# Query and projection on four 64x64 quadrants, with a group's images crossed between partition halves

## The chip, the cores and the metric

One core of one Trainium2 chip. The metric is device time in microseconds (us), from the start of the program to its end; several executions are timed and the median is compared. All data is float32.

## What is computed

A block of a convolutional network over 32 images of 64 channels and 16x16 pixels. Every step adds to its input:

```
x = x + conv_bn(x, dw0, groups=C)             # depthwise 3x3
x = x + ffn(x, f0)                            # 64 -> 128 -> relu -> 64
x = x + windowed_attn(x, ...)                 # 7x7 windows
x = x + conv_bn(x, dw1, groups=C)
x = x + ffn(x, f1)

def attn(xw):                                 # xw: windows, 49 tokens, 64 channels
    q = xw @ wq.T;  k, v = split(xw @ wkv.T);  k = k + pos
    q = focus((relu(q) + 1e-6) / sc);  k = focus((relu(k) + 1e-6) / sc)
    q, k, v = 4 heads of 16 channels
    z = 1 / (q . sum(k) + 1e-6)
    y = (q @ (k.T @ v)) * z + depthwise 5x5 of v
    return y @ proj_w.T + proj_b
focus(t) = t**3 / norm(t**3) * norm(t)
```

## The kernel before

The images go in eight groups of four. A group's tile has 128 partitions: channels of two images (index a, the partition half) times two images side by side in the columns (index j). So the four images of a group are (a, j). A window grid of 7x7 leaves four full windows of an image and a rest (right and bottom strips of 60 pixels).

**Slots.** Work is written out by hand for each engine, in slots n. Slot n runs the convolution and FFN of group n (of the first block; from slot 9 on, which has number n-1, those of the second block; slot 8 has none), queries, keys and values of group n-1, the key norms and key-value sums of groups n-2 and n-3, attention (attend, then take_y) of group n-5, y's turn to channels (turn_y) of group n-6, and the projection of group n-7. Slots 1 to 4 fill this up, with the convolution one group ahead. From slot 11 the rest of attention and the second block's end are written out singly.

**Order in a slot, PE** (TensorE; slots 6 to 10): conv, key_value_full, project, ffn1, attend, a window_conv in some (5, 6, 9), then query and ffn2 (in slots 5 and 6 ffn2 first), kv_rest, key_value_rest, q_norms, turn_y, kv_full. In slots 1 to 4: ffn1, conv, query, kv_full, kv_rest, key_value_rest, q_norms, ffn2.
**VectorE** (5 to 10): norm2, take_kv_full, norm6, ratios, take_y, k_focus, q_first, second, k_rest, k_full, k_guard, take_kv_rest. **ScalarE** (5 to 11): k_square, first, take_projected, k_sixth, hidden, take_fm, q_sixth, root, second, take_q_norms, take_v_rest, take_yt, take_v_full, q_square. **GpSimd** (POOL): add_pads, cube_k, third, y_sum, v_masks, cube_q. Each engine runs its list strictly in order; semaphores join them.

**Query** (L702, matmuls L719): for each partition half a one matmul of 64x64 weights over the 512 columns of both images, from half a to the same half of one PSUM bank (P_B + 1). **Project** (L875, L886) does the same into a spare convolution bank (groups 0 to 3) or P_B + 1. fp32 matmuls appear as two instructions each. So two of the four 64x64 quadrants of the array are in use. kv_full (L723, L734), kv_rest (L738), key_value_full (L780), key_value_rest (L800), attend (L808) and q_norms run over QUADRANTS (L139), all four.

**PSUM** has eight banks: 0 and 1 alternate for convolution and FFN output, P_H = 2, 3 hold the hidden layer, key rests and query norms, P_A = 4, 5 keys, values and attention, P_B = 6, 7 query, key-value sums, window convolution and turn_y. A step that reuses a bank waits for the engine that read it last.

**Afterwards.** q_first (L1045) takes the query from PSUM on VectorE; third adds the projection to x2, on POOL for groups 0 to 3 (L381, after ScalarE's take_projected, L523) and on VectorE for 4 to 7 (L1118). SP, the DMA queue, writes the result to mid in DRAM (L317) and reads it back by rows (L296) for the second convolution.

Of the kernel before, what the change touches and what calls it, by code (L numbers as in the profile page):

```python
# [8 lines left out]
ALU = mybir.AluOpType  # L9
# [126 lines left out]
def window_block_kernel(nc, x, taps_in, weights, consts, tables, out):  # L136
# [12 lines left out]
    with ExitStack() as ctx:  # L149
# [64 lines left out]
        vfull = sb("vfull", 128, NG, 8, VC)  # L214
# [7 lines left out]
        fm = sb("fm", 128, 2, NG, 4, C)  # L222
# [40 lines left out]
        def proj_bank(c):  # L263
            return spare(c + 7) if c < 4 else P_B + 1
# [70 lines left out]
        def _(eng):  # L335
# [37 lines left out]
            def y_sum(c):  # L373
                eng.wait_ge(y_ready, c + 1)
                eng.wait_ge(fm_ready, 3 if c < 4 else 6)
                full = y[:, c % 2, 0:8, :].rearrange("p (x s) c -> p x (s c)", x=2)
                eng.tensor_tensor(full, full, fm[:, :, c].rearrange("p x s c -> p x (s c)"), ALU.add)  # L377
# [35 lines left out]
        def _(eng):  # L413
# [19 lines left out]
            def take_v_full(g):  # L433
                eng.wait_ge(full_ps, g + 1)
                eng.wait_ge(kfull_ready, g + 1)
                eng.activation(vfull[:, g, :, 0:C], bank(P_A, 2).rearrange("p (s c) -> p s c", c=128)[:, :, C:128], ACT.Copy,  # L436
                               scale=cc("mask0")).then_inc(v_ready, 1)
# [64 lines left out]
            def take_fm(e):  # L502
# [3 lines left out]
                if part < 2:  # L506
                    for wx in range(2):
                        src = bank(P_B + wx).rearrange("p (d s h) -> p s d h", d=8, h=NH)
                        dst = fm[:, wx, gs, :, 32 * part:32 * part + 32].rearrange("p g s (d h) -> p (g s) d h", h=NH)
# [13 lines left out]
            def take_projected(c):  # L523
# [3 lines left out]
                eng.activation(xw[:, c % 2].rearrange("p j n -> p (j n)"), bank(proj_bank(c)), ACT.Identity,  # L527
# [92 lines left out]
        def _(eng):  # L620
# [4 lines left out]
            def conv(m, n, js=slice(0, GP)):  # L625
# [9 lines left out]
                if 0 <= n - 8 < 4:  # L635
                    eng.wait_ge(xw_ready, n - 7)
# [16 lines left out]
            def ffn1(m, n):  # L653
# [11 lines left out]
                if 0 <= n - 2 < NG:  # L665
                    eng.wait_ge(krest_ready, n - 1)
                if m == 13:
                    eng.wait_ge(y_ready, NG)
# [33 lines left out]
            def query(g, n):  # L702
# [14 lines left out]
                for a in range(2):  # L717
                    p = slice(64 * a, 64 * a + 64)
                    last = eng.matmul(bank(P_B + 1)[p].rearrange("p (j n) -> p j n", j=GP), ww("wq")[p], x2[p, g, :, 0:PX],  # L719
                                      start=True, stop=True)  # L720
# [17 lines left out]
            def kv_rest(g, n):  # L738
                eng.wait_ge(x2_ready, g + 1)
                if n < 5:  # L740
# [39 lines left out]
            def key_value_full(g, n):  # L780
# [10 lines left out]
                for j in range(GP):  # L791
                    for wy in range(2):
                        s = 2 * j + wy
                        for a, wx in QUADRANTS:
                            p = slice(64 * wx, 64 * wx + 64)
                            last = eng.matmul(bank(P_B + wx)[64 * a:64 * a + 64, VC * s:VC * s + VC], kf[p, g % 2, a, s, :],  # L796
                                              vfull[p, g, 4 * a + s, :], start=True, stop=True)
                last.then_inc(kvx_ps, 1)

            def key_value_rest(g):  # L800
                eng.wait_ge(vm_ready, g + 1)
                for a, j in QUADRANTS:
                    p = slice(64 * j, 64 * j + 64)
                    last = eng.matmul(bank(P_H + j)[64 * a:64 * a + 64, 0:5 * VC], kf[p, g % 2, a, 4, :],
# [553 lines left out]
```

## Time and profile before

| | |
|---|---|
| median of 3 runs | 174.64 us (173.4 to 175.21) |
| profiled execution | 174.51 us, span 172.7 us |
| PE busy | 157.2 us (91%) |
| VectorE, ScalarE, GpSimd busy | 103.9, 83.7, 57.5 us |
| mean granted clock of TensorE | 0.98 |
| DMA | 18.77 MB, mean 109 GB/s |

The span runs from the first to the last instruction of the profile; the execution's own time is longer by what lies around it. Shares of busy time are means over the whole span: the slots have different limits, so the rows below are read slot by slot. In a timeline a group's time is from its first start to its last end, and the next group can start before that end.

### The profile page before, as it was taken

How to read it: one execution, taken by the hardware profiler on the slowest of the kernel's cores; microseconds unless marked ns; L12 is line 12 of the kernel's file. 1: busy time of each engine (PE TensorE's matmuls, PEld its weight loads, DVE VectorE, ACT ScalarE, POOL GpSimd, SP SyncE). 2: the span in 40 equal slices, each digit the busy share in tenths (PEclk: the TensorE clock that was granted, in tenths of full speed). 3: DMA queues.
4: the chain of work that ended last, by engine and by line, in shares of the span. 5: the costliest groups of instructions: out<-in, count | busy, mean ns of one | idle time of the engine just before them, and what ended most of it. 6: DMA issues, size and time to landing. Idle time of an engine off the chain costs nothing. (4 is left out here: it accounts for less than half of the span.)

```text
span 172.7 us, 6668 instructions
## 1 busy us (share of the span) xinstructions
PE 157.2 (91%) x2840; PEld 76.6 (44%) x2840; DVE 103.9 (60%) x270; ACT 83.7 (48%) x178; POOL 57.5 (33%) x75
## 2 busy tenths in 40 slices
PE   6977999899898999999996789999989999987893
PEld 3312252627274873583383562576433425222231
DVE  1168263858777778597588586582189476606043
ACT  2054869494937665756745414653431414033132
POOL 4000028260825504263934926640254312000000
PEclk9999999999999999999999956999999999999999
DMA  5999999940000000000054161063027181959943
GB/s 144 291 245 292 212 215 208 206 84 6 0 4 4 4 4 4 0 4 4 28 141 78 66 143 35 4 171 72 4 76 163 63 173 66 189 167 218 299 140 121
DMA packets 18028, 18.77 MB, mean 109 GB/s; under 512 B 1104, under 2 KB 17744, under 8 KB 17872
## 3 DMA queue, kind: packets, MB, share of 16 engines
q1 hardware_dynamic: 17568, 17.83, 44.6%
q10 hardware_dynamic: 432, 0.52, 1.1%
q8 instruction: 22, 0.36, 0.9%
q14 instruction: 6, 0.05, 0.1%
HBM read 14.16 MB, written 4.19 MB: 106 GB/s over the span
## 5 line engine op out<-in xcount | busy, mean ns | idle before, releaser
L649 PE MATMUL ps<-xc,dwf 96*32 96x480 f32 (+3 forms) x408 | 44.9, 575 | 3.4 <-DMA xc<-mid 2.4
L371 POOL TENSOR_TENSOR qt<-q 128x512 f32<-128x512 f32 x8 | 10.7, 1333 | 57.2 <-ACT q L465 57.2
L649 PEld LDWEIGHTS ps<-xc,dwf 96*32 96x32 f32 x408 | 12.1, 112 | 32.7 <-issue 24.2
L424 ACT ACTIVATE x<-ps,wts 128x512 f32<-128x512 f32 x15 | 10.3, 685 | 26.0 <-PE ps L649 26.0
L671 PE MATMUL ps<-x,w1s 64*128 64x512 f32 x60 | 16.7, 637 | 2.9 <-DVE kvm L1107 1.4
L431 ACT ACTIVATE hid<-ps,wts 128x512 f32<-128x512 f32 x27 | 17.2, 682 | 3.2 <-PE ps L671 3.2
L677 PE MATMUL ps<-hid,w2s 128*64 128x512 f32 x60 | 17.2, 614 | 0.0
L377 POOL TENSOR_TENSOR y<-y,fm 128x512 f32<-128x512 f32 x8 | 10.2, 1274 | 10.7 <-DVE y L1161 7.7
L1061 DVE TENSOR_REDUCE nrm<-k 128x10 f32<-128x640 f32 x8 | 6.6, 819 | 11.6 <-ACT k L459 11.5
L358 POOL TENSOR_TENSOR k<-k 128x640 f32<-128x640 f32 x8 | 12.4, 1550 | 3.4 <-ACT k L453 3.4
L734 PE MATMUL ps<-wts,x 64*64 64x128 f32 x256 | 11.2, 294 | 0.6 <-DVE y L1161 0.6
L760 PEld LDWEIGHTS ps<-cst,q 64*64 64x64 f32 x512 | 10.8, 135 | 1.5 <-ACT q L473 0.9
L760 PE MATMUL ps<-cst,q 64*64 64x1 f32 x512 | 10.1, 192 | 0.3 <-ACT q L473 0.3
L734 PEld LDWEIGHTS ps<-wts,x 64*64 64x64 f32 x256 | 8.7, 143 | 3.5 <-issue 3.5
L719 PE MATMUL ps<-x,wts 64*64 64x512 f32 x32 | 8.6, 612 | 1.7 <-DVE kvm L1094 1.4
L364 POOL TENSOR_TENSOR vm<-vrest,cst 128x640 f32<-128x640 f32 x8 | 10.1, 1268 | 0.0
L671 PEld LDWEIGHTS ps<-x,w1s 64*128 64x128 f32 x60 | 4.6, 184 | 10.9 <-ACT x L424 5.8
L1112 DVE TENSOR_SCALAR hid<-ps,wts 128x512 f32<-128x512 f32 x3 | 2.3, 751 | 11.7 <-PE ps L671 11.6
L1094 DVE TENSOR_TENSOR kvm<-ps,cst 128x544 f32<-128x544 f32 x8 | 5.7, 717 | 5.6 <-PE ps L796 5.6
L1107 DVE TENSOR_TENSOR kvm<-ps,cst 128x680 f32<-128x680 f32 x8 | 6.9, 859 | 3.1 <-issue 2.3
L436 ACT ACTIVATE vfull<-ps,cst 128x512 f32<-128x512 f32 x8 | 5.5, 686 | 6.6 <-DVE kraw L1025 6.6
L459 ACT ACTIVATE k<-k 128x640 f32<-128x640 f32 x8 | 5.9, 736 | 5.7 <-POOL k L358 5.7
(139 smaller groups left out, 277.7 us busy)
## 6 DMA issues: line engine op xcount, KB each, us to landing
xc<-in_x SPq DMA_DIRECT2D x16, 240.0 KB, 11.4
xc<-mid SPq DMA_DIRECT2D x16, 240.0 KB, 4.7
xc<-in_x SPq DMA_DIRECT2D x8, 256.0 KB, 10.7
mid<-x SPq DMA_DIRECT2D x8, 256.0 KB, 2.2
xc<-mid SPq DMA_DIRECT2D x8, 256.0 KB, 3.3
out<-x SPq DMA_DIRECT2D x7, 256.0 KB, 5.7
tab<-in_tables SPq DMA_DIRECT2D x1, 1024.0 KB, 11.4
wts<-in_weights SPq DMA_DIRECT2D x1, 644.0 KB, 7.2
```

The lines of the kernel that those rows point to most:

```text
L358: eng.tensor_tensor(k3[:, :], k2[:, :], k1[:, :], ALU.mult).then_inc(k3_ready, 1)
L364: eng.tensor_tensor(vm[:, g % 2, :, :, 0:C], vrest[:, g].unsqueeze(2).broadcast_to([128, 2, 5, C]), cc("mask5").unsqueeze(1).unsqueeze(3). ...
L371: eng.tensor_tensor(qt[:, g % QB, 0:GC], q2[:, g % 2, 0:GC], q1[:, :], ALU.mult).then_inc(qt_ready, 1)
L377: eng.tensor_tensor(full, full, fm[:, :, c].rearrange("p x s c -> p x (s c)"), ALU.add)
L424: eng.activation(x1[:, m % 2, :], bank(m % 2), ACT.Identity, bias=ww(f"dwb_{m // NG}")).then_inc(x1_ready, 1)
L431: eng.activation(hid[:, m % 2, a, :], bank(hidden_bank(m) + a), ACT.Relu, bias=ww(f"fb1_{m // NG}")).then_inc(h_ready[a], 1)
L649: last = eng.matmul(out_ps[32 * q:32 * q + 32, :, :, to], dwf[:, s, q % 2, i, :], src[:, :, :, of], start=(i == 0), stop=False, skip_group ...
L671: eng.matmul(bank(hidden_bank(m) + a), w1s[p, s, :], x1[p, m % 2, :], start=True, stop=True).then_inc(h_ps, 1)
L677: last = eng.matmul(bank(m % 2)[64 * a:64 * a + 64], w2s[:, s, :], hid[:, m % 2, a, :], start=False, stop=True, skip_group_check=True)
L719: last = eng.matmul(bank(P_B + 1)[p].rearrange("p (j n) -> p j n", j=GP), ww("wq")[p], x2[p, g, :, 0:PX], start=True, stop=True)
L734: last = eng.matmul(bank(P_A + a)[64 * wx:64 * wx + 64, 128 * (2 * j + wy):128 * (2 * j + wy) + 128], x2[64 * a:64 * a + 64, g, j, at:at + ...
L760: eng.matmul(bank(P_H + a)[64 * h:64 * h + 64, at:at + 1], src[p, of:of + 64], one[p], start=True, stop=True)
```

## The change

Query and project run over all four quadrants, 256 columns each. A quadrant that leads from half a to half r carries image j = a ^ r, so two of the four images change their half between query and projection; project crosses them back. q is then spread over banks P_B and P_B + 1, 256 columns in each, and the projection over two banks: P_H, P_H + 1 for groups 0 to 3, a spare convolution bank with P_B + 1 for 4 and 5, P_A, P_A + 1 for 6 and 7. Key-value sums go to crossed halves, and vfull, fm and the window convolution's operands are reordered to match.

The waits follow the banks: turn_y waits for q_first of its slot, project for the last users of P_H, ffn1 for take_projected, convolutions 11 and 12, project(7) and ffn1(13) for third. In PE's order attend moves ahead of ffn1 in slots 6 to 10; in VectorE's, q_first moves ahead of take_y (slots 7 and 8) or directly behind it (slots 5 and 6).

```diff
-        def proj_bank(c):
-            return spare(c + 7) if c < 4 else P_B + 1
+        def proj_banks(c):
+            if c < 4:
+                return P_H, P_H + 1
+            return (spare(9 + c), P_B + 1) if c < 6 else (P_A, P_A + 1)
...
-                eng.activation(vfull[:, g, :, 0:C], bank(P_A, 2).rearrange("p (s c) -> p s c", c=128)[:, :, C:128], ACT.Copy,
+                eng.activation(vfull[:, g // 4, :, g % 4, 0:C], bank(P_A, 2).rearrange("p (s c) -> p s c", c=128)[:, :, C:128], ACT.Copy,
...
-                eng.activation(xw[:, c % 2].rearrange("p j n -> p (j n)"), bank(proj_bank(c)), ACT.Identity,
+                eng.activation(xw[:, c % 2], bank(P_H, 2).rearrange("p (j n) -> p j n", j=GP)[:, :, 0:PX], ACT.Identity,
...
(conv)
-                if 0 <= n - 8 < 4:
-                    eng.wait_ge(xw_ready, n - 7)
+                if m in (11, 12):
+                    eng.wait_ge(x3_ready, m - 6)
...
(ffn1)
+                if 0 <= n - 7 < 4:
+                    eng.wait_ge(xw_ready, n - 6)
                 if m == 13:
-                    eng.wait_ge(y_ready, NG)
+                    eng.wait_ge(x3_ready, NG)
...
(query)
-                for a in range(2):
-                    p = slice(64 * a, 64 * a + 64)
-                    last = eng.matmul(bank(P_B + 1)[p].rearrange("p (j n) -> p j n", j=GP), ww("wq")[p], x2[p, g, :, 0:PX],
-                                      start=True, stop=True)
+                for a, r in QUADRANTS:
+                    j = a ^ r
+                    last = eng.matmul(bank(P_B + j)[64 * r:64 * r + 64, 0:PX], ww("wq")[64 * a:64 * a + 64],
+                                      x2[64 * a:64 * a + 64, g, j, 0:PX], start=True, stop=True)
...
(kv_rest)
+                if n == NG:
+                    eng.wait_ge(xw_ready, 2)
...
(key_value_full)
-                            last = eng.matmul(bank(P_B + wx)[64 * a:64 * a + 64, VC * s:VC * s + VC], kf[p, g % 2, a, s, :],
-                                              vfull[p, g, 4 * a + s, :], start=True, stop=True)
+                            last = eng.matmul(bank(P_B + wx)[64 * (a ^ j):64 * (a ^ j) + 64, VC * s:VC * s + VC], kf[p, g % 2, a, s, :],
+                                              vfull[p, g // 4, 4 * a + s, g % 4, :], start=True, stop=True)
...
(window_conv)
-                            src = vfull[p, gs, :, NH * dc:NH * dc + NH].rearrange("p g (a j y) h -> p (g a) j y h", a=2, j=2)[:, :, j]
+                            src = vfull[p, half, :, :, NH * dc:NH * dc + NH].rearrange("p (a j y) g h -> p a j (y g) h", a=2, j=2)
+                            src = src[:, ::-1, j] if j else src[:, :, j]
...
(turn_y)
+                if n <= NG:
+                    eng.wait_ge(q_ready, n)
...
(project)
                 if c < 4:
-                    eng.wait_ge(x2_ready, nextconv(n) - 1)
-                else:
+                    eng.wait_ge(kvr_ready, n - 3)
+                    eng.wait_ge(qn_ready, min(n - 2, NG))
+                    eng.wait_ge(krest_ready, min(n - 1, NG))
+                elif c < 6:
+                    eng.wait_ge(x2_ready, c + 6)
                     eng.wait_ge(kvx_ready, NG)
                     eng.wait_ge(fm_ready, 6)
-                    if c > 4:
+                    if c == 5:
                         eng.wait_ge(x3_ready, c)
-                for a in range(2):
-                    p = slice(64 * a, 64 * a + 64)
-                    last = eng.matmul(bank(proj_bank(c))[p], ww("proj")[p], yt[p, c % 2, :], start=True, stop=True)
+                else:
+                    eng.wait_ge(y_ready, NG)
+                    if c == 7:
+                        eng.wait_ge(x3_ready, c)
+                for r, a in QUADRANTS:
+                    j, p = r ^ a, slice(64 * r, 64 * r + 64)
+                    last = eng.matmul(bank(proj_banks(c)[j])[64 * a:64 * a + 64, 0:PX], ww("proj")[p],
+                                      yt[p, c % 2, PX * j:PX * j + PX], start=True, stop=True)
...
(PE's order)
                         project(n - 7, n)
+                    attend(n - 5, n)
                     if m is not None:
                         ffn1(m, n)
-                    attend(n - 5, n)
...
(q_first)
-                eng.tensor_scalar(q1[:, :], bank(P_B + 1), 0.0, ecol[:, 0:1], ALU.max, ALU.add).then_inc(q_ready, 1)
+                eng.tensor_scalar(q1[:, :].rearrange("p (j n) -> p j n", j=GP), bank(P_B, 2).rearrange("p (j n) -> p j n", j=GP)[:, :, 0:PX],
+                                  0.0, ecol[:, 0:1], ALU.max, ALU.add).then_inc(q_ready, 1)
...
(VectorE's order)
                 ratios(n - 2)
+                if n in (7, 8):
+                    q_first(n - 1)
                 take_y(n - 5)
+                if n in (5, 6):
+                    q_first(n - 1)
                 if n - 2 < NG:
                     k_focus(n - 2)
-                if n - 1 < NG:
-                    q_first(n - 1)
```

## Rows read from the trace of the kernel before

**Rows 1.** The profile's first part: busy us, share of span, instructions.

```profile
PE 157.2 (91%) x2840; PEld 76.6 (44%) x2840; DVE 103.9 (60%) x270; ACT 83.7 (48%) x178; POOL 57.5 (33%) x75
```

**Rows 2.** Stretches, slots 7, 8: length, busy us (instructions), PE clock, DMA share, GB/s.

```profile
78.20:90.60 12.40, 12.40 (x274) 6.34 (x270) 9.44 (x22) 7.91 (x18) 7.51 (x10) 1.00 0.20 58
90.60:103.00 12.40, 9.12 (x242) 6.10 (x236) 9.38 (x22) 4.94 (x11) 7.51 (x10) 0.88 0.41 92
```

**Rows 3.** Stretches, columns as before, finer behind slot 8.

```profile
99.90:103.00 3.10, 2.48 (x42) 1.81 (x38) 2.64 (x8) 0.60 (x1) 0.47 (x1) 0.52 0.72 163
103.00:106.70 3.70, 3.70 (x24) 0.99 (x24) 3.11 (x4) 1.83 (x3) 1.50 (x3) 0.50 0.40 72
```

**Rows 4.** Waits of PE: us in total, times, longest us.

```profile
PE ps L719 <- DVE kvm L1094: 1.4, 1, 1.4
PE ps L671 <- DVE kvm L1107: 1.4, 2, 0.7
```

**Rows 5.** The chain that ended last, one piece: start, us, what.

```profile
144.12 2.15 DMA mid<-x
```

**Rows 6.** PE in time order: start, us, line, operation, count [idle before <-releaser].

```profile
21.79 0.65 PE L719 MATMUL ps<-x,wts 64*64 64x512 f32 x2
...
23.42 0.28 PE L747 MATMUL ps<-wts,x 64*64 64x128 f32 x2
...
61.17 0.65 PE L719 MATMUL ps<-x,wts 64*64 64x512 f32 x2 [0.30 <-ACT fm L510]
...
62.71 0.69 PE L760 MATMUL ps<-cst,q 64*64 64x1 f32 x31
...
86.53 0.45 PE L747 MATMUL ps<-wts,x 64*64 64x128 f32 x8
86.79 0.75 PE L804 MATMUL ps<-vm,kf 64*64 64x340 f32 x8
87.36 0.59 PE L760 MATMUL ps<-cst,q 64*64 64x1 f32 x32
...
108.01 1.02 PE L886 MATMUL ps<-yt,wts 64*64 64x512 f32 x4
108.97 1.13 PE L671 MATMUL ps<-x,w1s 64*128 64x512 f32 x4
```

**Rows 7.** PE in order of time, slots 6 to 8.

```profile
76.16 0.90 PE L773 MATMUL ps<-cst,y 128*64 128x98 f32 x16
...
89.62 1.10 PE L734 MATMUL ps<-wts,x 64*64 64x128 f32 x32
...
101.09 1.98 PE L734 MATMUL ps<-wts,x 64*64 64x128 f32 x32 [0.62 <-DVE y L1161]
```

**Rows 8.** VectorE in order of time, slots 6 to 8.

```profile
75.00 0.28 DVE L1161 TENSOR_TENSOR y<-ps,den 128x128 f32<-128x128 f32 x1
...
88.43 0.28 DVE L1161 TENSOR_TENSOR y<-ps,den 128x128 f32<-128x128 f32 x1
...
100.67 0.28 DVE L1161 TENSOR_TENSOR y<-ps,den 128x128 f32<-128x128 f32 x1
...
101.60 0.74 DVE L1049 TENSOR_SCALAR q<-ps,ecol 128x512 f32<-128x512 f32 x1
```

**Rows 9.** ScalarE in order of time, hidden layer of slots 9 and 10.

```profile
110.29 1.26 ACT L431 ACTIVATE hid<-ps,wts 128x512 f32<-128x512 f32 x2
...
124.47 1.26 ACT L431 ACTIVATE hid<-ps,wts 128x512 f32<-128x512 f32 x2 [0.36 <-PE ps L671]
```

**Rows 10.** PE in order of time, slots 9 and 10.

```profile
112.26 1.08 PE L677 MATMUL ps<-hid,w2s 128*64 128x512 f32 x4
...
123.31 1.13 PE L671 MATMUL ps<-x,w1s 64*128 64x512 f32 x4
...
125.51 1.35 PE L677 MATMUL ps<-hid,w2s 128*64 128x512 f32 x4
...
129.34 0.70 PE L823 MATMUL ps<-kvm,qt 64*64 64x68 f32 x32 [0.66 <-DVE y L1161]
```

More of the change, by code:

```diff
@@ L213, in window_block_kernel @@
         kf = sb("kf", 128, 2, 2, 5, C)
-        vfull = sb("vfull", 128, NG, 8, VC)
+        vfull = sb("vfull", 128, 2, 8, 4, VC)
         vrest = sb("vrest", 128, NG, 2, C)
@@ L221, in window_block_kernel @@
         y = sb("y", 128, 2, 10, C)
-        fm = sb("fm", 128, 2, NG, 4, C)
+        fm = sb("fm", 128, 2, 2, 4, 4, C)
         fmr = sb("fmr", 128, NG, 2, C)
@@ L375, in y_sum @@
                 eng.wait_ge(fm_ready, 3 if c < 4 else 6)
-                full = y[:, c % 2, 0:8, :].rearrange("p (x s) c -> p x (s c)", x=2)
-                eng.tensor_tensor(full, full, fm[:, :, c].rearrange("p x s c -> p x (s c)"), ALU.add)
+                full = y[:, c % 2, 0:8, :].rearrange("p (x s) c -> p x s c", x=2)
+                eng.tensor_tensor(full, full, fm[:, :, c // 4, :, c % 4], ALU.add)
                 rest = y[:, c % 2, 8:10, :]
@@ L508, in take_fm @@
                         src = bank(P_B + wx).rearrange("p (d s h) -> p s d h", d=8, h=NH)
-                        dst = fm[:, wx, gs, :, 32 * part:32 * part + 32].rearrange("p g s (d h) -> p (g s) d h", h=NH)
+                        dst = fm[:, wx, half, :, :, 32 * part:32 * part + 32].rearrange("p s g (d h) -> p (s g) d h", h=NH)
                         last = eng.activation(dst, src, ACT.Copy)
@@ L803, in key_value_rest @@
                     p = slice(64 * j, 64 * j + 64)
-                    last = eng.matmul(bank(P_H + j)[64 * a:64 * a + 64, 0:5 * VC], kf[p, g % 2, a, 4, :],
+                    last = eng.matmul(bank(P_H + j)[64 * (a ^ j):64 * (a ^ j) + 64, 0:5 * VC], kf[p, g % 2, a, 4, :],
                                       vm[p, g % 2, a].rearrange("p w c -> p (w c)"), start=True, stop=True)
@@ L860, in window_conv @@
                             last = eng.matmul(bank(spare(n))[p, 32 * dc:32 * dc + 32], trest[p, dc, :],
-                                              vrest[p, gs, :, NH * dc:NH * dc + NH].rearrange("p g a h -> p (g a) h"),
+                                              vrest[p, gs, ::1 - 2 * k, NH * dc:NH * dc + NH],
                                               start=True, stop=True)
@@ L1121, in third @@
                 eng.wait_ge(mid_out, 16 * (c - 1))
-                dst, src = x3[:, c % 2, :], bank(proj_bank(c))
+                dst = x3[:, c % 2, :]
                 for j in range(GP):
+                    src = bank(proj_banks(c)[j])
                     for wx in range(2):
-                        at = PX * j + 98 * wx
+                        at = 98 * wx
                         eng.scalar_tensor_tensor(natural(dst, j)[:, 0:14, WR * wx:WR * wx + WR],
@@ L1129, in third @@
                 for j in range(GP):
-                    at = PX * j + WIN
+                    src, at = bank(proj_banks(c)[j]), WIN
                     eng.scalar_tensor_tensor(natural(dst, j)[:, :, 14:16], src[:, at:at + 32].rearrange("p (h w) -> p h w", w=2),
@@ L1213, in _ @@
             eng.tensor_copy(ecol[:, :], bank(P_B)[:, 0:1]).then_inc(ecol_ready, 1)
-            eng.tensor_copy(vfull[:, :, :, C:VC].rearrange("p g s h -> p (g s) h"),
+            eng.tensor_copy(vfull[:, :, :, :, C:VC].rearrange("p b s g h -> p (b s g) h"),
                             cc("mask0").unsqueeze(2).broadcast_to([128, NG * 8, NH]))
```

## The prediction

> **What bounds the kernel now.** The page's first part comes first: TensorE (PE) is busy for 157.2 of 172.7 us [rows 1], so shorter matmuls look like time won. The second view, the stretches by slot, asks whether that holds everywhere. In slot 7 PE is busy for all 12.40 us; in slot 8, which has no convolution, for 9.12 of 12.40 [rows 2]. The reader should see that VectorE does 9.4 us in both, so slot 8 is as long as slot 7 with 3.3 us less of PE work: another chain sets its length. That chain is one group's keys: kv_full (PE), k_full and k_guard (VectorE), k_square (ScalarE), cube_k (GpSimd), k_sixth (ScalarE), norm6, ratios, take_y (VectorE), and back to the next kv_full, which waits for the last y. The third view is the granted clock: it was 0.52 and 0.50, the lower of its two levels, from about 99.9 to 106.7 us, just behind slot 8's idle time [rows 3]. Fourth, the waits of PE: query waits 1.4 us for VectorE's key-value copy (slot 8), ffn1 waits twice 0.7 us for the other one (slots 4 and 5) [rows 4]. Last, the chain that ended last: from 144.12 us on it is nearly all DMA, beginning with the write of group 5 to mid, which third(5) on VectorE releases [rows 5]. So the end moves by as much as project(5) and third(5) do, and what is saved behind them (projections 6 and 7) counts for nothing.
>
> **One query or projection.** Now four instructions of 512 columns run on two quadrants; project holds PE from 108.01 to 108.97, 0.96 us [rows 6]. After it, eight of 256 columns run on four. The nearest row is key_value_rest, eight instructions of 340 columns on four quadrants, 86.79 to 87.36: 0.57 us [rows 6]. 256 columns can't cost more if the four overlap as there, and in proportion they cost 0.43. I take 0.45, as the work is columns, and keep 0.43 to 0.57. A project so saves 0.5, and a query at most as much.
>
> One condition differs from key_value_rest: there each half of the array's rows has a bank of its own; here both halves write to each of the two banks, in different partition halves. The old project does the same, both halves into one bank, and its four instructions of 0.6 us mean overlap within 1.02 us [rows 6], so the sharing does not stop them. The Trainium skill ("TensorEngine Tiling (Array Packing)", Gotcha 1: PSUM Pressure) says that different row tiles cannot use one PSUM bank at the same time. By that rule the new pairs would take turns and each call would stay near 0.96 us; the row speaks against it, for disjoint partitions at least. It is rival 4.
>
> **Slots 1 to 4.** Before, kv_full already fills the quadrants that query leaves empty: from the first query matmul to the end of both is 23.42 - 21.79 = 1.63 us [rows 6], where kv_full alone lasts 1.10 [rows 7]. After: 0.45 + 1.10 = 1.55, less a little overlap at the seam (project lasts 1.02 and its successor starts after 0.96). I take 0.15 saved for each. Slots 2 and 3 are paced by VectorE, which comes to k_full only behind k_focus and q_first of the same slot, with PE waiting for its copies [rows 4], so two of the four reach the end: 0.3 (bounds 0.1 and 0.6).
>
> **Slot 5.** Query, kv_rest and key_value_rest take 62.71 - 61.17 = 1.54 us interleaved; the last two alone 87.36 - 86.53 = 0.83 [rows 6]. After: 0.45 + 0.83 = 1.28. Saved: 0.26.
>
> **Slot 6.** ffn2 is held by the hidden layer, which ScalarE reaches only behind k_sixth; moving attend ahead of ffn1 changes nothing there. Query would give 0.26 again, but turn_y now waits for q_first, since query writes its bank too, and behind turn_y stands kv_full. q_first follows take_y, which ends at 75.00 + 0.28, and lasts 0.74 [rows 8]: 76.02, where turn_y began at 76.16 [rows 7]. Saved: 0.15. k_focus moves back by 0.74; its reader, the next slot's key_value_full, has a whole convolution in front of it, so that costs nothing.
>
> **Slots 7 and 8.** q_first is moved ahead of take_y. It was already in VectorE's order, but behind the y that kv_full waits for; now it lies in front, inside the key chain. In slot 7 the last y was written at 88.71 [rows 8], so it comes at 89.45, and kv_full, which began at 89.62 [rows 7], gains 0.15 at most, though PE has 1.0 us less to do. In slot 8 kv_full was already waiting (0.62 us) for the y of 100.95 [rows 7, 8]; there 0.74 goes straight on the path. I take -0.7. The new waits of project in slot 8 (it must see the last key-value copy of slot 7) hold attend and query too, but query stood for 1.4 us anyway [rows 4], and 0.45 + 1.1 fits in that.
>
> **Slots 9 and 10.** attend now runs before ffn1, so ScalarE copies the projection under it (half of the 1.26 us that two such copies take [rows 9], under attend's 1.1, from ffn1's end at 124.44 to 125.51 [rows 10]) and ffn1's new wait costs nothing. But attend was also the cover of the hidden layer, 1.26 us of ScalarE between ffn1 and ffn2. Slot 9: project ends 0.5 earlier, ffn1 starts at 108.97 - 0.5 + 1.1 = 109.6 and ends at 110.7, hidden at 112.0, and ffn2 ends 1.1 later, as in slot 10 (126.86 against 125.73): 113.1 against 113.34 [rows 6, 9, 10]. Saved: 0.2. In slot 10 nothing else stands between ffn1 and ffn2: ffn1 starts 0.6 later, at 123.9, so ffn2 ends 0.6 later too. In return take_y starts 1.6 earlier, and the 0.66 us that attend(6) waited for it [rows 10] go. Net: 0.05.
>
> **Slots 11 and 12.** PE is busy throughout up to project(5); projections 4 and 5 give 0.5 each: 1.0. The new waits for third are covered: third(5) was done at 144.1 [rows 5], and the convolution that must wait for it stood behind four more PE steps. Copies, masks and the relabelled operands keep their element counts: 0.
>
> **Sum.** 0.3 + 0.26 + 0.15 + 0.15 - 0.7 + 0.2 + 0.05 + 1.0 = 1.4 us. The profiled execution took 174.51 us (span 172.7 plus 1.81 around it), 0.13 below the median shown; 174.51 - 1.4 = **173.1 us**.
>
> **Rivals.**
> 1. *The saving reaches the end everywhere.* PE is 91% busy. Four queries at 0.15, three at 0.26, one (slot 7, no interleaving) at 0.5 and six projections at 0.5 make 4.9: 169.6 us. Against it stands slot 8, where missing PE work did not shorten the slot. Chance 0.10.
> 2. *The slow clock goes or shrinks.* It cost kv_full 1.98 - 1.10 = 0.88 [rows 7], and 3.7 us at half rate behind it another 1.85 [rows 3]: 2.7. If the idle stretches fall otherwise, all of it may go: 173.1 - 2.7 = 170.4; half, 171.7. Against it: slot 8 idles more, not less. Chance 0.15.
> 3. *A second slow stretch, and slower.* Slot 7 loses 1.0 us of PE work and little of its length, so PE stands idle there as it did before the clock fell behind slot 8. It decides if the granted clock falls at the end of slot 7 too: that costs another 2.7, 175.8. Against it: by my sum slot 7 idles 0.9 us, slot 8 idled 3.3. Chance 0.15.
> 4. *The quadrants take turns.* Calls stay at 0.96, nothing is saved, and the reordering remains: in slot 7, 9 and 10 ffn1 comes 1.1 later (some 0.35, 0.3 and 0.45 lost), in slot 8 -0.7: 174.51 + 1.8 = 176.3. The old project speaks against it. Chance 0.07.
>
> **How the numbers follow.** The forecast has the other 0.53. Its own range: with 0.57 for a call the sum falls to about 0.5 (174.0); with nothing lost in slot 8 it is 2.1 (172.4); so 172.2 to 174.1. From 170.8 to 175.9 the range leaves out rival 1, rival 4 and the lowest part of rival 2, about 2 in 10. The runs before differ by about 1%, which is what can be told from no change: below 172.9 is faster, above 176.4 slower. Faster: rivals 1 and 2 and two fifths of the forecast, 0.46. Slower: half of rival 4, a little of rival 3, and 0.03 for what I don't see: 0.09. Same: 0.45.
>
> **What would show it.** Query and project at 0.43 to 0.57 us, all four quadrants overlapping; slots 7 and 8 each about 12.3 us from kv_full to kv_full, with PE waiting for y in both; attend(6) without a wait; ffn2 in slot 10 waiting for the hidden layer; third(5) about 1.4 us earlier. The prediction is wrong if slot 8 gets shorter at the full clock, if a stretch at 0.5 is missing or a second appears, or if third(5) moves and the end does not.

## The result, and the profile after

The changed kernel is a little slower. Its median is 178.16 us over 20 runs, 174.97 us for the kernel before in as many; the medians hold disturbed executions (12 of the changed kernel's 20), which the ratio leaves out: 1.0103, with a 95% interval of 1.0061 to 1.0145. The forecast of 173.1 us (170.8 to 175.9) missed. The profiled execution took 175.90 us with a span of 174.0 us, 1.3 us longer than the span before.

The page's first part and the granted clock in 40 slices (in tenths of full speed), changed kernel:

```profile
PE 154.8 (89%) x2904; PEld 78.5 (45%) x2904; DVE 102.8 (59%) x270; ACT 84.1 (48%) x178; POOL 57.4 (33%) x75
PEclk9999999999999999999999858999999999969999
```

PE is busy for 2.4 us less than in [rows 1], though it has 64 more matmuls and 64 more weight loads. The clock falls twice where it fell once. Stretches of the changed kernel, columns as in [rows 2]: slots 7 and 8, then the parts at the lower clock.

```profile
77.80:90.30 12.50, 12.26 (x294) 6.87 (x293) 9.48 (x23) 7.91 (x18) 7.52 (x10) 1.00 0.21 58
90.30:102.90 12.60, 8.69 (x244) 6.62 (x235) 9.32 (x22) 5.05 (x11) 7.51 (x10) 0.83 0.29 69
98.60:102.00 3.40, 2.77 (x36) 2.43 (x40) 3.25 (x12) 0.60 (x1) 1.24 (x2) 0.50 0.08 20
102.00:105.40 3.40, 3.40 (x36) 1.38 (x32) 2.12 (x3) 1.37 (x3) 0.09 (x1) 0.50 1.04 217
153.10:156.00 2.90, 2.88 (x16) 0.81 (x20) 0.00 (x0) 0.00 (x0) 0.00 (x0) 0.52 0.43 139
```

The stretch behind slot 8 answers to [rows 3]; the one at 153.1 is new. What PE did before it stands in its waits (us in total, times, longest; "issue" means that it waited for nothing that the profile shows), changed kernel:

```profile
PE ps L651 <- DMA xc<-mid: 3.2, 1, 3.2
PE ps L902 <- issue: 1.9, 1, 1.9
PE ps L681 <- ACT hid L433: 1.2, 3, 0.8
PE ps L651 <- issue: 0.5, 1, 0.5
```

PE stands once for 3.2 us, waiting for the rows that conv(13) reads back from mid; before, the same line had three waits, none over 1.0 us. The chain that ended last (start, us, what), changed kernel, says why those rows came late:

```profile
143.88 3.76 DMA mid<-x
...
148.50 4.57 DMA xc<-mid
...
153.12 4.37 PE ps L651 x24
```

third(5) releases the write of group 5 at 143.88, 0.24 us earlier than in [rows 5], but it lands after 3.76 us, not 2.15. The read behind it is late by that, and conv(13) starts behind the read and runs at the lower clock: 4.37 us, where a convolution at the full clock takes 2.68. The DMA view of the write, packets by queue, first the kernel before (144.0 to 147.5 us), then the changed one (143.8 to 147.7):

```profile
GB/s 0 0 0 0 0 0 0 0 0 0 0 94 293 363 363 339 363 351 351 316 153 12 0 0 0 0 0 0 0 0 0 0 0 0 0 0 47 82 82 23
q1 hardware_dynamic: 292, 0.28, 25.9%
```

```profile
GB/s 0 0 0 0 0 0 0 0 0 11 263 357 315 347 357 336 336 273 221 0 0 0 0 0 0 0 0 11 11 11 11 0 0 0 0 0 0 0 0 0
q1 hardware_dynamic: 272, 0.26, 20.2%
q8 instruction: 1, 0.02, 1.4%
```

The bulk of the write takes as long in both. In the changed kernel nothing of the write moves for some 0.8 us (each figure is a slice of 0.1 us) and then a trickle of 11 GB/s ends it: in the packets, 15 of the write's 16 shares (each ends with a packet of 4 bytes) have ended by 145.66 us and the last at 146.91, behind a 16 KB load of instructions on queue 8 (145.58 to 146.46 us). Over the whole program queue 8 has 23 such loads, 22 before. PE's stream, the list of instructions that it works off, has 2904 matmuls and as many weight loads now, 2840 of each before: an estimate of 250 to 260 such entries for a load.

PE in order of time, changed kernel, parts of slots 1, 6 to 8, 9 and 10, then the same part of slot 10 before:

```profile
22.71 0.66 PE L723 MATMUL ps<-x,wts 64*64 64x256 f32 x8
23.19 1.05 PE L738 MATMUL ps<-wts,x 64*64 64x128 f32 x32
...
75.74 0.90 PE L779 MATMUL ps<-cst,y 128*64 128x98 f32 x16 [0.27 <-DVE q L1066]
...
89.09 1.10 PE L738 MATMUL ps<-wts,x 64*64 64x128 f32 x32
...
101.20 1.98 PE L738 MATMUL ps<-wts,x 64*64 64x128 f32 x32 [0.55 <-DVE y L1180]
...
107.35 0.61 PE L902 MATMUL ps<-yt,wts 64*64 64x256 f32 x8
107.78 0.65 PE L829 MATMUL ps<-kvm,qt 64*64 64x68 f32 x32
...
118.20 1.04 PE L651 MATMUL ps<-xc,dwf 96*32 96x512 f32 x2
119.74 2.67 PE L651 MATMUL ps<-xc,dwf 96*32 96x512 f32 x22 [0.49 <-issue]
...
122.86 0.61 PE L902 MATMUL ps<-yt,wts 64*64 64x256 f32 x8
...
126.28 1.65 PE L681 MATMUL ps<-hid,w2s 128*64 128x512 f32 x4 [0.77 <-ACT hid L433]
```

```profile
119.23 2.68 PE L649 MATMUL ps<-xc,dwf 96*32 96x512 f32 x24
...
122.36 1.02 PE L886 MATMUL ps<-yt,wts 64*64 64x512 f32 x4
```

The calls are as short as forecast: query holds PE for 23.19 - 22.71 = 0.48 us, project for 107.78 - 107.35 = 0.43. But conv(9) breaks off after 2 of its 24 matmuls and goes on at 119.74: its two matmuls should have ended near 118.6, and no engine is named as the one that held it. From its start to project it takes 122.86 - 118.20 = 4.66 us, against 3.13 (122.36 - 119.23) before: 1.5 us lost in the middle of a convolution that no named wait holds. The 4,802nd entry of PE's stream (here semaphore instructions count too) is the one that comes late; a 16 KB load began at 116.91 and ended at 118.23. The 1.9 us of L902 in the waits above, in slot 8, are another matter: project goes on at 92.69 us, 0.10 us after VectorE has written the key-value copy that it waits for (91.73 to 92.59).

So the span's 1.3 us come from three parts. To the first convolution: 9.25 us against 8.26, +1.0. From there to the end of third(5): 134.61 (143.86 - 9.25) against 135.84, -1.2, with the broken conv(9) in it. From there to the end of the chain: 27.97 against 26.46, +1.5. The first part can't be put down to the change: one and the same kernel further down (the kernel before with fill, run twice) had its first convolution at 9.23 and at 8.40.

### The profile page after: what moved, and what is told of

Read it like the earlier page. It is cut to its first block and busy times, and to the rows that moved or that the text cites. A ratio compares the mean times of both kernels' runs of the same rounds, so it can differ in the third digit from the quotient of the medians.

```text
span 174.0 us, 6802 instructions
## 1 busy us (share of the span) xinstructions
PE 154.8 (89%) x2904; PEld 78.5 (45%) x2904; DVE 102.8 (59%) x270; ACT 84.1 (48%) x178; POOL 57.4 (33%) x75
## 5 line engine op out<-in xcount | busy, mean ns | idle before, releaser
L651 PE MATMUL ps<-xc,dwf 96*32 96x480 f32 (+3 forms) x408 | 46.7, 584 | 4.6 <-DMA xc<-mid 3.2
L651 PEld LDWEIGHTS ps<-xc,dwf 96*32 96x32 f32 x408 | 13.0, 114 | 34.4 <-issue 27.7
L681 PE MATMUL ps<-hid,w2s 128*64 128x512 f32 x60 | 18.4, 614 | 1.2 <-ACT hid L433 1.2
L379 POOL TENSOR_TENSOR y<-y,fm 128x512 f32<-128x512 f32 x8 | 10.2, 1269 | 11.9 <-DVE y L1180 8.9
L766 PEld LDWEIGHTS ps<-cst,q 64*64 64x64 f32 x512 | 9.8, 135 | 2.8 <-ACT q L475 1.3
L766 PE MATMUL ps<-cst,q 64*64 64x1 f32 x512 | 9.5, 192 | 0.7 <-ACT q L475 0.7
L738 PE MATMUL ps<-wts,x 64*64 64x128 f32 x256 | 9.5, 290 | 0.6 <-DVE y L1180 0.6
L675 PEld LDWEIGHTS ps<-x,w1s 64*128 64x128 f32 x60 | 4.6, 184 | 10.2 <-issue 6.9
L625 PE MATMUL ps<-x 128*128 128x512 f32 x12 | 7.9, 824 | 1.5 <-DVE x L1183 1.5
L738 PEld LDWEIGHTS ps<-wts,x 64*64 64x64 f32 x256 | 8.1, 144 | 1.7 <-issue 1.2
L523 ACT ACTIVATE yt<-ps 128x512 f32<-128x512 f32 x8 | 4.8, 597 | 8.4 <-PE ps L783 8.4
```

The costliest lines, as they stand in the source:

```text
L379: eng.tensor_tensor(full, full, fm[:, :, c // 4, :, c % 4], ALU.add)
L625: eng.matmul(bank(P_B + 1), x1[:, 0, 0:128], x1[:, 0, :], start=True, stop=True)
L651: last = eng.matmul(out_ps[32 * q:32 * q + 32, :, :, to], dwf[:, s, q % 2, i, :], src[:, :, :, of], start=(i == 0), stop=False, skip_group ...
L675: eng.matmul(bank(hidden_bank(m) + a), w1s[p, s, :], x1[p, m % 2, :], start=True, stop=True).then_inc(h_ps, 1)
L681: last = eng.matmul(bank(m % 2)[64 * a:64 * a + 64], w2s[:, s, :], hid[:, m % 2, a, :], start=False, stop=True, skip_group_check=True)
L738: last = eng.matmul(bank(P_A + a)[64 * wx:64 * wx + 64, 128 * (2 * j + wy):128 * (2 * j + wy) + 128], x2[64 * a:64 * a + 64, g, j, at:at + ...
```

## The experiments

The theory after the two traces: the slots gain as forecast, and it is lost again because the change adds 8 entries to PE's stream with each query and project (88 ahead of conv(9), 112 up to and with projection 5). So the instruction loads fall elsewhere: PE waits for one in conv(9), another delays the write of group 5, and behind that write the clock falls. The rivals: the lower clock alone (slot 8, tail), or the change's own order.

**The changed kernel again.**

> The changed kernel once more. Theory A (the clock): PE stands idle longer in slot 8 and before convolution 13, the granted clock falls to 0.5 in both places, and the stretches together cost more than the 1.4 us saved; ratio to before 1.005 to 1.02, and the profile has two stretches at 0.5, one from about 99 us and one from about 150 us. Theory B (order and DMA): the loss is the late landing of group 5's write (3.76 us instead of 2.15) and the pause of 1.2 us in convolution 9, both of which then show again, whatever the clock does.

Measured: 176.5 us, ratio 1.0144 [1.0087, 1.0201]. conv(9) breaks at the same matmul (118.35 x2, then 119.89), the write lands in 4.03 us, the clock falls in both places, conv(13) takes 5.13 us. So none of these is an accident of one execution.

**Hold the clock up.** Matmuls on constants into a free bank, in places where PE stands idle: in slot 8 (first), ahead of conv(13) and conv(14) (second), in both (third).

```diff
+            def fill(b, k):
+                for _ in range(k):
+                    eng.matmul(bank(b)[:, 0:PX], cc("ident"), tab[:, 0:PX], start=True, stop=True)
...
+                    if n == 8:
+                        fill(0, 4)
                     if n >= 7:
                         project(n - 7, n)
...
+            fill(P_B, 4)
             conv(13, 14)
...
```

> The changed kernel with seven extra matmuls of 256 columns (128x128 weights, constants, result never read) in PE's idle places of slot 8: four before project, one each before q_norms, turn_y and kv_full. Theory A: the clock stays high through slot 8 and convolution 8 runs in 2.7 us instead of 3.8 to 4.5; 2 to 2.7 us faster than the changed kernel, ratio to before about 0.995. Theory B: no faster than the changed kernel, slower by up to 0.5 us where a filler is longer than the wait.

> The changed kernel with four such matmuls between convolutions 12 and 13 and two before convolution 14, where PE waits for the rows read back from mid. Theory A: no stretch at 0.5 in the tail, convolution 13 in 2.7 us instead of 4.4; 1.5 to 2 us faster than the changed kernel. Theory B: the same time or slower by up to 0.5 us, since the DMA sets the end.

> The changed kernel with the fillers of slot 8 and of the tail together. Theory A: 3.5 to 4.5 us faster than the changed kernel, about 172 us, ratio to before about 0.985, and a mean granted clock above 0.98. Theory B: 0 to 1 us slower than the changed kernel.

Measured: 176.56 us, ratio 1.0078 [1.0028, 1.0128]; 175.86 us, 1.0105 [1.0054, 1.0156]; 175.45 us, 0.9966 [0.9918, 1.0014]. PE in order of time, first kernel:

```profile
102.05 2.68 PE L651 MATMUL ps<-xc,dwf 96*32 96x512 f32 x24
...
117.43 0.45 PE L858 MATMUL ps<-vfull,tab 64*64 64x64 f32 x11 [1.40 <-issue]
117.80 2.68 PE L651 MATMUL ps<-xc,dwf 96*32 96x512 f32 x24
```

All three gained less than expected. Each fill does its part and no more. With slot 8 filled, the convolution behind it runs at the full clock (2.68 us, where it began at the lower one in [rows 3]), but in the tail the clock still falls, and for longer: 10.2 us (149.9 to 160.1), 3.4 in the changed kernel's first profile. With the tail filled, conv(13) takes 2.68 us, but the clock falls in slot 8. With both the mean clock is 1.00, and by the ratios (1.0144 to 0.9966, same chip) that is worth 1.8%, 3.1 us. What the clock does not explain stays: the write lands in 3.73 to 4.18 us in all three. And with slot 8 filled the pause moves: the fill adds 28 entries ahead of it, so that the late entry no longer lies in conv(9) but in the window convolution just before it. It goes with the count of entries, not with a line of the program.

**Move the loads.** 43 one-column matmuls in place of one of the opening ones (172 entries for 4, as a float32 matmul is two matmul entries and two weight loads), in the changed kernel; the same with 29 in the kernel before; and with 36 and both fills in the changed kernel.

```diff
+            for i in range(43):
+                a, r = QUADRANTS[i % 4]
+                eng.matmul(bank(P_A + a)[64 * r:64 * r + 64, 0:1], x1[64 * a:64 * a + 64, 0, 0:64], x1[64 * a:64 * a + 64, 0, 0:1],
+                           start=True, stop=True)
-            for _ in range(6):
+            for _ in range(5):
```

> The changed kernel; one of the six opening matmuls is replaced by 43 of one column, so PE's stream holds 168 instructions more before its first convolution and every later instruction lies 168 places further on; nothing else is changed. Theory C (instruction loads): PE's instructions come in loads of 16 KB, 256 instructions each; one now falls on convolution 9 and one on group 5's write. Moved by 168 they fall elsewhere: convolution 9 without its pause (1.4 us), the write lands after about 2.2 us instead of 3.8 to 4.2, end 2 to 3 us earlier, ratio to before about 0.995 to 1.0. Theory A (the clock alone): pause and late landing stay, or their going changes nothing; ratio 1.01 to 1.015.

> The kernel before, its stream shifted in the same way by 112 instructions, as many as query and projection add up to project(5). Theory C: it takes on the changed kernel's loads: a pause of about 1.4 us in convolution 9 or the window convolution ahead of it, group 5's write landing after 3.7 us or later, 2 to 3 us slower than before, ratio 1.01 to 1.02. Theory A: ratio 1.00, since no work and no idle time of a slot is changed.

> The changed kernel with the fillers of slot 8 and the tail, and the stream shifted by 140 instructions ahead of the first convolution, so that with slot 8's 28 it lies 168 further on from convolution 9. Theories A and C together: clock high throughout, no pause, early landing: 5 to 6 us faster than the changed kernel, about 171 us, ratio about 0.975. Theory A alone: as with the fillers only, 0.997. Theory C alone: as with the shift only, about 0.995.

Measured: 175.11 us, ratio 0.9991 [0.9954, 1.0028]; 185.19 us, without a ratio; 177.46 us, 1.0145 [1.0093, 1.0198]. In the first, conv(9) is whole and the write lands in 2.14 us, PE in order of time:

```profile
10.64 2.68 PE L655 MATMUL ps<-xc,dwf 96*32 96x512 f32 x24
...
118.52 2.68 PE L655 MATMUL ps<-xc,dwf 96*32 96x512 f32 x24
```

It gains 1.1% on the changed kernel although its first convolution starts 1.4 us later; that delay came with the edit. The clock has a part in this, though: in this profile it stays at 1.00 in slot 8, though PE stands for 1.9 and 1.4 us there, and falls only in conv(13). The second has pauses of 1.8 and 1.2 us with the releaser "issue" in slot 3 and ahead of conv(9), and its write lands in 4.06 us, but it lost 10 us where 2 to 3 were expected, its first convolution began 2.5 us later, and the clock fell in four places: it settles nothing. The third missed as well: a pause of 1.9 us appeared in slot 3, in q_norms, with a stretch at the lower clock behind it. A shift that clears two places can put the pause in a third.

**Move the loads where PE is idle.** 18 one-column matmuls behind conv(0) and 24 behind conv(1), of constants, in the changed kernel (168 entries).

```diff
+            def tiny(k):
+                for i in range(k):
+                    a, r = QUADRANTS[i % 4]
+                    eng.matmul(bank(P_A + a)[64 * r:64 * r + 64, 0:1], cc("ident")[64 * a:64 * a + 64, 64 * a:64 * a + 64], cc("one")[64 * a:64 * a + 64],
+                               start=True, stop=True)
...
             conv(0, 0)
+            eng.wait_ge(c_in, 16)
+            tiny(18)
             ffn1(0, 0)
             conv(1, 1)
+            tiny(24)
```

> The changed kernel with 42 matmuls of one column (168 instructions) where PE waits anyway, behind its first two convolutions, instead of ahead of the first one; no other change. Theory C: the loads lie as with the shift before, without the 1.4 us that the shift cost at the start: conv 9 without a pause, write of group 5 landing after 2.2 us, ratio to before 0.985 to 0.995, and any rest above that is the clock's. Theory A alone: 1.01.

Measured: 173.22 us, ratio 0.9886 [0.982, 0.9953], 2.2% below the changed kernel by the ratios. PE in order of time and a piece of its chain:

```profile
118.77 2.68 PE L651 MATMUL ps<-xc,dwf 96*32 96x512 f32 x24
...
121.90 0.61 PE L902 MATMUL ps<-yt,wts 64*64 64x256 f32 x8
```

```profile
142.92 2.15 DMA mid<-x
```

The kernel has 42 useless matmuls more and is faster. conv(9) to project is 3.13 us again; the write lands in 2.15. The lower clock behind slot 8 is still there (99.0 to 105.8); the fall in the tail is gone without any fill: PE's longest wait for a read from mid is 2.0 us there, not 3.2. From the write of group 5 to the end of the chain it now takes 26.4 us, as in the kernel before.

**The reverse: the loads of the changed kernel in the kernel before.** One-column matmuls behind conv(0) (18), conv(1) (26) and ahead of attend(6) (12), and nothing of the change.

> The kernel before with 56 one-column matmuls more (112 entries in PE's stream, as many as the change adds ahead of projection 5), put where PE stands idle: 18 behind conv(0), 26 behind conv(1), 12 ahead of attend(6). Nothing of the change is in it. Theory (the place of PE's instruction loads makes the loss): conv(9) starts some of its matmuls, then stands for 1.0 to 1.6 us with no wait named, as in the changed kernel; a 16 KB load falls on the write of group 5, which lands in 3.7 us or more instead of 2.15; the median is 1 to 3 us above the kernel before (ratio 1.006 to 1.017). Rival (the loss comes from the change's own order, q_first ahead of take_y and the new waits): no pause, the write lands in 2.15 us, ratio within 0.995 to 1.005.

Measured: 181.1 us, ratio 1.0315 [1.0229, 1.0401]. A pause of 1.5 us came, in the window convolution ahead of conv(9), but the write landed in 2.14 us with no load in it: half a hit. Not all of the loss is the stream's: the twelve matmuls ahead of attend(6) last 2.8 us, where PE had waited 0.7 before, and the clock falls behind them (135.5 to 138.9 us). Two short pauses in slot 5 cost another 1.7 (conv(5) to conv(6): 21.34 us, 19.64 before). The expectation counts wrongly: 56 such matmuls are 224 entries, not 112. So the next two have the count right: 9, 13 and 6 in the kernel before; 6, 10 and 6 in the kernel before with the six fill matmuls of slot 8 (told below).

> The kernel before with half of the last kernel's additions: 9 one-column matmuls behind conv(0), 13 behind conv(1), 6 ahead of attend(6). A float32 matmul is two matmul entries and two weight loads in PE's stream, so the 56 of the last kernel were 224 entries; these 28 are 112, 88 ahead of conv(9) and 112 ahead of projection 5, as in the change. Theory (place of the instruction loads): a pause of 1.0 to 1.6 us inside conv(9) within a few matmuls of where the changed kernel has it, the write of group 5 lands in 3.7 to 4.2 us with a 16 KB load in it, ratio 1.006 to 1.02. Rival (the change's own order makes both): conv(9) in one piece, the write in 2.15 us, ratio 0.995 to 1.005.

> The kernel before with the fill matmuls of slot 8 (24 entries), 16 one-column matmuls behind conv(0) and conv(1) and 6 ahead of attend(6): again 88 entries more ahead of conv(9) and 112 ahead of projection 5, with the clock held up in slot 8. Theory: pause in conv(9) and a write of 3.7 to 4.2 us as above; beside the kernel before with fill alone (0.984 to 0.986) it loses 1 to 3 us: ratio 0.990 to 1.003. Rival: as the kernel with fill alone, 0.982 to 0.988.

Measured: 184.75 us, ratio 1.0528 [1.0446, 1.061]; 178.66 us, 1.0185 [1.0122, 1.0247]. PE in order of time and its chain, the second kernel (with fill):

```profile
118.47 1.05 PE L649 MATMUL ps<-xc,dwf 96*32 96x512 f32 x5
120.73 2.66 PE L649 MATMUL ps<-xc,dwf 96*32 96x512 f32 x19 [1.21 <-issue]
...
123.85 0.60 PE L886 MATMUL ps<-yt,wts 64*64 64x512 f32 x2
```

```profile
146.31 3.88 DMA mid<-x
```

and of the first:

```profile
124.83 1.05 PE L649 MATMUL ps<-xc,dwf 96*32 96x512 f32 x5
126.75 2.66 PE L649 MATMUL ps<-xc,dwf 96*32 96x512 f32 x19 [0.87 <-issue]
```

Here nothing of the change is in the kernel, and conv(9) breaks at the same entry of PE's stream, the 4,802nd, in both kernels (3 matmuls further on, as the matmuls lie a little differently). With fill, conv(9) to project takes 5.38 us, 2.25 over the whole one, and the write lands in 3.88 us with an instruction load from 148.19 to 149.14 in it. That refutes the rival that the change's own order makes the pause and the late write. Both lost more than expected, and the added matmuls have a part in it: the six ahead of attend(6) hold PE for 1.4 us, where it had waited 0.7. In the other kernel the load starts only at 154.32, 0.5 us before the write ends, which lands in 2.54 us: a part. Its loss of 5% has mostly another pause behind it, 4.8 of the 7.6 us by which its span is longer (conv(3) to conv(5): 23.59 us, 18.77 before): in slot 3, PE in order of time,

```profile
37.33 0.39 PE L764 MATMUL ps<-cst,q 64*64 64x1 f32 x8 [2.96 <-issue]
37.65 1.98 PE L677 MATMUL ps<-hid,w2s 128*64 128x512 f32 x4
```

3.0 us without an instruction, and then a stretch at the lower clock (36.3 to 43.1 us).

Over all 15 profiles of this study and the two that it set out from, the write of group 5 landed in 2.13 to 2.15 us in the nine that have no instruction load inside it, and in 3.73 to 4.18 in the seven where one ran while it was under way; the 2.54 above is the one between. Six of the seven were the two changed and the three filled kernels and the shifted kernel before; the seventh had nothing of the change either. The kernel before bears this out too, in its last write, group 7's:

```profile
152.36 3.77 DMA mid<-x
```

A load runs from 153.13 to 154.60 us, inside it; the same write takes 2.17 to 2.21 us in the seven other profiles whose chain shows it without a load, and 3.54 in the one other with a load. But there it costs nothing: from group 5's write to the end it is 26.4 us with it, and 26.4 in the kernel of 42 idle matmuls without it.

The pauses have a rule as well, which the count of entries shows. Over all these profiles PE stands 20 times for 0.2 us or more with no wait named (project in slot 8 aside), and each time the late entry is the 706th, 1,986th, 2,242nd, 3,522nd, 3,778th or 4,802nd of its stream, to within one, whatever instruction that is. These places lie 256 entries, or a multiple of 256, apart. So a pause stands at a fixed place of the stream, and added entries decide which work lies there.

**What the change is worth when both are out of the way.** Fill in slot 8 alone, in the kernel before (three ahead of query, one each ahead of q_norms, turn_y and kv_full); and in the changed kernel, with the 42 one-column matmuls, fill in slot 8 and the tail. Each was run on its own first, then both side by side.

> The kernel before with fillers in its idle places of slot 8: three matmuls of 256 columns before query, one each before q_norms, turn_y and kv_full (24 instructions). Theory A: its one stretch at 0.5 goes, 2 to 2.7 us faster, ratio about 0.987, unless the 24 instructions move a load onto dense work. Theory C: no gain from the clock, ratio 1.00, or slower by the pause.

> The same with fillers: in slot 8 two matmuls of 512 columns before project and one of 256 before each of q_norms, turn_y and kv_full (20 instructions), in the tail four and one of 256. Theories A and C: no pause, no late landing, no stretch at 0.5; what is left is the change itself, 1 to 2 us faster than the kernel before with its fillers (ratio 0.984), so 0.972 to 0.979. If the change gives nothing by itself: 0.984.

> The kernel before with the fill matmuls in slot 8 only, beside the last one on one chip. Both theories: ratio 0.982 to 0.987, full clock throughout, the write of group 5 landing in 2.1 to 2.2 us. It is the mark for the kernel ahead of it.

> The changed kernel with the 42 one-column matmuls and the fill matmuls in slot 8 and the tail, as before, now beside the next kernel on one chip. Theory: the change is worth its 1.2 us once loads and clock are out of the way, so this one is 0.5 to 1.2 us faster than the kernel before with fill: ratio 0.978 to 0.982 against 0.984. Rival: what the change saves is lost in slot 8 and in the transfers behind group 5, so both come out within 0.3 us of each other.

Measured: 172.16 us, ratio 0.9841 [0.9798, 0.9885]; 171.26 us, 0.9815 [0.9765, 0.9865]; then side by side 172.74 us, 0.9857 [0.9782, 0.9931], and 171.80 us, 0.9823 [0.9766, 0.9881]. Both beat both kernels. The clock held up in slot 8 is worth 1.4 to 1.6% to the kernel before (the fill also moves its stream by 24 entries). The change on top of it is 0.9 us by the medians of one chip, as expected, but the intervals overlap: that it gains at all is not settled by these runs.

## Why the prediction was wrong

Time saved (us, from the starts of convolutions and third(5)'s end), forecast and measured: before against after, and in the last pair of kernels, at full clock and with conv(9) whole in both. The pair flatters the change from conv(7) to conv(8): there the fill itself holds kv_full back in the kernel before, 0.81 us behind the last y (101.45 to 102.26), where it was 0.14 without fill. And of the pair's 2.78 us, 1.57 is lost ahead of conv(2) (21.12 us against 19.55, with the 42 one-column matmuls in it) and 0.35 in the tail, which leaves 0.9.

| stretch | forecast | before to after | pair with fill |
|---|---|---|---|
| conv(0) to conv(5) (pair: from conv(2)) | 0.3 | 0.76 | 0.68 |
| conv(5) to conv(6) | 0.26 | 0.56 | 0.93 |
| conv(6) to conv(7) | 0.15 | 0.08 | 0.10 |
| conv(7) to conv(8) | -0.55 | -0.51 | 0.12 |
| conv(8) to conv(9) | 0.2 | 1.13 | 0.20 |
| conv(9) to conv(10) | 0.05 | -1.32 | 0.23 |
| conv(10) to third(5) | 1.0 | 0.53 | 0.52 |
| sum | 1.4 | 1.23 | 2.78 |

**One call** was right: 0.43 to 0.48 us against 0.45. The quadrants overlap although both halves write to one bank, so rival 4 is out. The Trainium skill ("TensorEngine Tiling (Array Packing)", Gotcha 1: PSUM Pressure) says that different row tiles cannot use one bank at the same time; for disjoint partition halves the trace disagrees, with eight instructions of 0.38 us each begun and ended within 0.61 us.

**Slots 1 to 5** were undersized (0.56 forecast, 1.3 measured): a query there saves 0.42 us and not 0.15. From its first matmul to ffn2 it was 2.10 us (21.79 to 23.89) and is 1.68 (22.71 to 24.39); the forecast's sum broke off at 23.42, where kv_rest begins while kv_full still runs. Slot 2 passes on next to nothing of it, slot 3 0.25. **Slots 6 and 7** came as told: turn_y waits for q_first (0.27 us at 75.74), and little is saved. But kv_full did not wait for y in slot 7, as the signs had it. **Slot 8** was right in size and cause: from kv_full to kv_full 101.20 - 89.09 = 12.11 us (12.12 in the pair's changed kernel, at the full clock), 11.47 before [rows 7], so 0.64 lost against 0.7, with q_first in front of take_y on VectorE and PE waiting for y. The new wait of project there (1.9 us) stands in place of query's 1.4 [rows 4], as told. **Slot 9**: the 1.13 is mostly the clock, which rose again at 105.4 us here and at 106.7 before [rows 3]; the pair has the 0.2. **Slot 10** was right: attend(6) does not wait any more, and ffn2 waits 0.77 us for the hidden layer. **Slots 11 and 12** gave half. "PE is busy throughout up to project(5)" fails in slot 11, where ffn1 stood behind project and now waits 0.21 us for ScalarE's share of conv(10): 0.12 of project(4)'s 0.5 arrives.

In the sum these errors nearly cancel: that third(5) came 1.23 us earlier, counted from conv(0), where 1.4 was forecast, is luck. Between the forecast of 1.4 us less and the span's 1.3 more, 1.0 is the start, 1.5 the tail and 0.2 the middle, in which conv(9)'s loss hides behind what slots 1 to 5 and the clock of slot 9 gave. **The step that failed** is the costing of the calls by their columns alone: "eight of 256 columns run on four", with the doubled number of instructions at nothing. The term that is missing is the 112 stream entries: 1.5 us in conv(9), and a write of group 5 that lands 1.6 us later. The second also broke the sentence that the end moves by as much as project(5) and third(5) do: third(5) was 0.24 us earlier and the end 1.3 us later. Late write and lower clock can be told apart there: from the write's start to the end of the chain it takes 27.6 and 27.8 us where the write is late and the clock held up (the two kernels with the tail filled), 27.2 where the write is whole and the clock falls (the first shifted kernel), 28.0 in the changed kernel with both, and 26.4 with neither. For conv(9) and the write, shown by taking the entries' effect away (2.15 us, whole conv(9), 0.9886) and by making it without the change (3.88 us, broken conv(9), 1.0185).

**Rival 3**, a second slow stretch, happened in kind, but in the tail behind a wait for DMA and not in slot 7, whose clock stayed at 1.00. **Rival 2** had its worth right: the clock of slot 8 gives 1.4 to 1.6% to the kernel before, 2.5 to 2.8 us, where 2.7 was worked out. But the change does not remove that stretch. **Rival 1** is not borne out. With loads moved, the changed kernel's 173.2 us is close to the forecast, but that is another kernel than the one asked about, with other gains and losses in it.

Left open: which of the places 256 entries apart make PE wait. Most go unnoticed; the pauses came in or behind q_norms, window convolutions and attend, runs of many short matmuls, but not behind all of them, and not in each execution: one profile of the changed kernel with both additions has 4.3 us in q_norms of slot 3 (that execution took 177.22 us, the other six 170.41 to 172.17), the other profile of the same kernel has none there. Open too is the start: the first convolution began between 8.3 and 9.9 us in kernels whose opening was not touched.

## What to carry to other kernels

Splitting a matmul into more and shorter ones is paid in entries of the instruction stream too, and where these move the loads of instructions can matter more than the columns saved: count the entries ahead of each point, and look for pauses with no wait named and for instruction loads beside a transfer that sets the end. Before a change of 1% is judged, run it with a few idle matmuls put in early: a shift of the stream by 112 to 224 entries went with 2% less in one of these two kernels and up to 5% more in the other, the added matmuls' own time included. And look where the clock falls behind idle time; a handful of matmuls there (1.4 to 1.6%) was worth more than what the change was meant to bring (0.8%).

## What the runs showed of the hardware

- A load of instructions is 16 KB (0.38 MB in 23), and PE goes on 2.2 to 3.1 us after the load ahead of its pause has begun, over all 20 pauses (116.91 to 119.74; 117.86 to 120.73; 123.86 to 126.75 us). The Trainium skill ("Runtime: NRT & Kernel Launch", Instruction fetch mechanics) gives blocks of 16 KiB or 256 instructions, which agrees with the 256 entries between the pauses. It says that crossing a block is mostly hidden; here PE stood idle for 0.2 to 4.3 us at such a place, 20 times in 17 profiles.
- One such load of 0.9 to 1.7 us inside a write of 256 KB in 16 shares makes it land 1.6 to 2.0 us later: the write is as late as its last share (146.91 us, the other 15 by 145.66).
- The granted clock fell to 0.50, the lower of its two levels, behind PE's idle time in slot 8, behind the 3.2 us of waiting ahead of conv(13) and behind the pause in slot 3, and stayed there for 3.4 to 10.2 us while PE was busy again. The length of one wait does not decide it: ahead of conv(13) it fell behind 2.39 us in the first shifted kernel and did not behind 2.44 in the kernel before with fill and 112 entries. With matmuls on constants in PE's idle places it stayed at 1.00 to the last matmul in four profiles: of the changed kernel with both fills, of the kernel before with fill (twice), and of the last changed kernel.
